# Neighbourhood attention and MLP on one core: x and the result held by channel, 16-bit row maxima through a step-zero column

## What is computed

```python
h1 = n1_w * arcsinh(x) + n1_b
h  = x + na2d(h1)                      # qkv, softmax over 9 neighbours, projection
h2 = n2_w * arcsinh(h) + n2_b
out = h + gelu(h2 @ mlp_w1 + mlp_b1) @ mlp_w2 + mlp_b2

def na2d(x):
    q, k, v = split(x @ qkv_w + qkv_b)
    scores = einsum('bijnd,bijmnd->bijnm', q * hd**-0.5, k[neighbours])
    return einsum('bijnm,bijmnd->bijnd', softmax(scores), v[neighbours]) @ proj_w + proj_b
```

## Time and profile before

| | |
|---|---|
| median of 3 runs | 4412.26 us |
| profiled execution: span | 4410.1 us |
| TensorE matmul busy | 4291.9 us (97%) |
| TensorE weight loads busy | 3082.4 us (70%) |
| VectorE busy | 3769.7 us (85%) |
| ScalarE busy | 3660.2 us (83%) |
| GpSimd busy | 3450.6 us (78%) |
| granted TensorE clock, mean | 0.992 |
| DMA, mean | 136 GB/s |

### The profile page before, as it was taken

The page is one execution under the profiler, slowest core; times in us unless marked ns, Lnnn a source line. Parts: engine busy times, 40 slices in busy tenths (PEclk is TensorE's granted clock), DMA queues, the critical chain, the costliest instruction groups (busy, mean ns, idle before and its releaser), DMA issues.

```text
span 4410.1 us, 136683 instructions
## 1 busy us (share of the span) xinstructions
PE 4291.9 (97%) x53320; PEld 3082.4 (70%) x53320; DVE 3769.7 (85%) x7715; ACT 3660.2 (83%) x5377; POOL 3450.6 (78%) x4092
## 2 busy tenths in 40 slices
PE   5999999999999999999999999999999999999997
PEld 3677777767777777776777777777777767777775
DVE  5888888888888888888888888888888888888884
ACT  4888888888888888888888888888888888888884
POOL 2787887888788788888878878887887888788775
PEclk8999999999999999999999999999999999999998
DMA  4555555555555555555555555555555555555551
GB/s 118 130 137 144 136 139 139 141 140 138 140 140 137 143 136 139 139 139 140 138 144 135 138 141 139 140 138 142 136 138 139 140 139 139 141 139 137 140 134 51
DMA packets 593555, 600.06 MB, mean 136 GB/s; under 512 B 76558, under 2 KB 540560, under 8 KB 590352
## 3 DMA queue, kind: packets, MB, share of 16 engines
q1 hardware_dynamic: 592912, 591.32, 51.4%
HBM read 197.69 MB, written 135.40 MB: 76 GB/s over the span
## 4 chain that ended last, share of the span: by engine, by line
DVE 42%; PE 34%; issue 12%; POOL 11%; SPq 1%; ACT 1%; DMA 0%; POOLq 0%; DVEq 0%; ACTq 0%
PE ps L382 32%; DVE ln_u L777 8%; DVE ln_u L773 8%; POOL a_lo L1162 6%; DVE o_norm L882 6%; DVE ps L851 5%; POOL a_hi L1160 3%; DVE q_nat L818 2%; DVE y L845 2%; DVE recip L873 2%; DVE v_nat L832 2%; PE ps L406 2%; DVE o_lo L838 2%; DVE ln_u L770 1%; DVE maxima L857 1%
## 5 line engine op out<-in xcount | busy, mean ns | idle before, releaser
L1154 POOL TENSOR_TENSOR p_lo<-prob,p_hi 100x512 f16<-100x512 f32 x1024 | 1256.7, 1232 | 639.1 <-ACT p_hi L1072 639.1
L1071 ACT ACTIVATE prob<-ps 100x512 f32<-100x512 f32 x1024 | 613.6, 599 | 143.2 <-PE ps L382 141.8
L882 DVE TENSOR_TENSOR o_norm<-ps,recip 64x128 f32<-64x128 f32 x2048 | 591.3, 289 | 49.4
L1180 POOL TENSOR_TENSOR g_lo<-g,g_hi 128x512 f16<-128x512 f32 x512 | 595.9, 1164 | 41.0
L1072 ACT ACTIVATE p_hi<-ps 100x512 f16<-100x512 f32 x1024 | 617.2, 603 | 0.0
L382 PEld LDWEIGHTS ps<-v_win,p_hi 100*128 100x128 f16 x8192 | 484.7, 98 | 185.3 <-issue 15.3
L851 DVE TENSOR_REDUCE ps<-ps 128x8 f32<-128x800 f32 x512 | 509.5, 995 | 88.9 <-PE ps L382 84.8
L382 PE MATMUL ps<-w_hi,g_hi 128*128 128x256 f16 x2048 | 560.3, 274 | 0.0
L382 PE MATMUL ps<-w_lo,g_hi 128*128 128x256 f16 x2048 | 560.2, 274 | 0.0
L382 PE MATMUL ps<-w_hi,g_lo 128*128 128x256 f16 x2048 | 560.1, 273 | 0.0
L382 PE MATMUL ps<-v_win,p_hi 100*128 100x65 f16 x8192 | 516.5, 194 | 26.0 <-POOL p_lo L1154 15.8
(11 more groups left out here) (103 smaller groups left out, 11981.0 us busy)
## 6 DMA issues: line engine op xcount, KB each, us to landing
keys<-k_win SPq DMA_DIRECT2D x1536, 100.0 KB, 2.2
v_win<-v_rows SPq DMA_DIRECT2D x1024, 101.6 KB
queries<-q_nat SPq DMA_DIRECT2D x1536, 64.0 KB
v_rows<-v_nat SPq DMA_DIRECT2D x256, 260.0 KB, 5.6
xin<-in_x_dram SPq DMA_DIRECT2D x128, 512.0 KB, 4.5
out_dram<-y SPq DMA_DIRECT2D x256, 256.0 KB, 3.1
queries<-in_query_mask_dram SPq DMA_DIRECT2D x128, 160.0 KB
keys<-in_mlp_w_dram SPq DMA_DIRECT2D x2, 512.0 KB, 7.5
```

The lines of the kernel that those rows point to most:

```text
L882: s = v.tensor_tensor(o_norm[r, c], av[r, :, HD * e:HD * e + HD], recip[c % 2][r].to_broadcast([NQ, PAIRS, HD]), ALU.mult)
L1071: act.activation(prob[b][0:NK], ps[0:NK, B_ST + b, :], ACT.Exp, scale=INV * INV).then_inc(prob_ready, 1)
L1154: pool.tensor_tensor(p_lo[b][0:NK], prob[b][0:NK], p_hi[b][0:NK], ALU.subtract).then_inc(p_lo_ready, 1)
L1180: pool.tensor_tensor(g_lo[:, m, :], g32[:, m, :], g_hi[:, m, :], ALU.subtract).then_inc(g_lo_ready, 1)
```

## The change

x reaches the device with channels on partitions: the host lays it out as (band, 128, 2, 512), and takes the result back in the same form. The eight x transposes, their copies and the eight transposes of h are gone; x is no longer held times 16. A load goes straight into one of five `xT` buffers (before: four, and one input buffer). `mlp_out` makes the result with channels on partitions, 24 matmuls of 512 columns, with the weight as the stationary operand; h is added by VectorE, in `result`, after `h_plus_bias` has added the bias to it in place. The banks of v, of the result and of the waits on them are handed out anew. The projection weight's scale goes from 16 to 4, and its counterpart, the ones beside v, from 1 to 4.

VectorE writes the maxima as one bf16 number in SBUF, and `subtract_max` multiplies a stationary operand that is one column read 128 times (step zero) with minus the identity. The second bf16 part, the transpose and the copy are gone.

```diff
-XT = 4
+XT = 5
-X_BANK = [1, 0]
-V_BANK = [2, 1]
-OUT_BANK = [2, 0]
+V_BANK = [1, 2]
+OUT_BANK = [0, 2]
...
-                if has(t + 4):
-                    sp.wait_ge(pe_x, signals(t + 3, G, G))
+                if t >= 0 and has(t + 4):
+                    if has(t - 1):
+                        sp.wait_ge(h_ready, signals(t - 1, G, G))
                     load_x(t + 4)
...
             def v_product(t, n):
-                if n == 0:
+                if n == 1:
                     pe.wait_ge(q_lo_ready, signals(t, G, 1))
-                elif has(t + 1):
-                    pe.wait_ge(xT_ready, signals(t + 1, G, 1))
-                else:
+                elif has(t - 3):
                     pe.wait_ge(h_ready, signals(t - 3, G, 2))
...
             def mlp_in(t, m):
                 if m == 0 and has(t - 1):
+                    pe.wait_ge(y_ready, signals(t - 1, 2, 2))
+                elif m == 0:
+                    pe.wait_ge(v_lo_ready, signals(t + 3, 2, 2))
+                elif m == 1 and has(t - 1):
                     pe.wait_ge(y_ready, signals(t - 1, 2, 1))
-                elif m == 0:
-                    pe.wait_ge(v_lo_ready, signals(t + 3, 2, 1))
-                elif m == 1 and has(t - 1):
-                    pe.wait_ge(y_ready, signals(t - 1, 2, 2))
...
-            def mlp_out(t, par, n):
+            def mlp_out(t, g):
...
-                for k in range(2):
-                    tok = slice((2 * n + k) * P, (2 * n + k + 1) * P)
-                    o = ps[:, OUT_BANK[n], k * C:(k + 1) * C]
-                    for g in range(G):
-                        pe.matmul(o[:, g * P:(g + 1) * P], h[par][:, g, tok], ident[:], start=(k == 0 and g == 0),
-                                  stop=False, is_transpose=True, skip_group_check=True)
-                    for m in range(MT):
-                        s = three(o, [g_[:, m, tok] for g_ in (g_hi, g_lo)], [w[:, m, :] for w in (w2_hi, w2_lo)],
-                                  False, m == MT - 1)
+                for m in range(MT):
+                    s = three(ps[:, OUT_BANK[g], :], [w[:, m, g * P:(g + 1) * P] for w in (w2_hi, w2_lo)],
+                              [g_[:, m, :] for g_ in (g_hi, g_lo)], m == 0, m == MT - 1)
                 s.then_inc(pe_m2, 1)
...
-                    s = mm(ps[:, B_ST + c % 2, p * P:(p + 1) * P], key_max[:, (c % 2) * PAIRS + p, :], max_row[k % 2][:],
-                           stop=True)
+                    a = maxima[k % 2][:, c % 2, p:p + 1]
+                    column = bass.AP(a.tensor, a.offset, [list(a.ap[0]), [0, P]])
+                    s = mm(ps[:, B_ST + c % 2, p * P:(p + 1) * P], column, minus_ident[:], stop=True)
...
             def magnitude_plus_root(u, root, s):
-                v.scalar_tensor_tensor(out=u, in0=u, scalar=INV, in1=root, op0=ALU.mult, op1=ALU.add).then_inc(s, 1)
+                v.tensor_tensor(u, u, root, ALU.add).then_inc(s, 1)
...
-            def result(t, n):
-
-                v.wait_ge(pe_m2, signals(t, 2, n + 1))
-                v.wait_ge(y_out[n], signals(t, 16, 0))
-                v.scalar_tensor_tensor(out=y[n][:], in0=ps[:, OUT_BANK[n], :].rearrange("p (k c) -> p k c", c=C), scalar=INV,
-                                       in1=b2[:].rearrange("p (a c) -> p a c", a=1).to_broadcast([P, 2, C]),
+            def h_plus_bias(t, par):
+                v.wait_ge(asinh2, signals(t, 1, 1))
+                for g in range(G):
+                    v.tensor_scalar(h[par][:, g, :], h[par][:, g, :], b2[:, g:g + 1], None, ALU.add).then_inc(hb_ready, 1)
+
+            def result(t, par, g):
+
+                v.wait_ge(pe_m2, signals(t, 2, g + 1))
+                v.wait_ge(y_out[g], signals(t, 16, 0))
+                v.wait_ge(hb_ready, signals(t, G, g + 1))
+                v.scalar_tensor_tensor(out=y[g][:], in0=ps[:, OUT_BANK[g], :], scalar=INV, in1=h[par][:, g, :],
                                        op0=ALU.mult, op1=ALU.add).then_inc(y_ready, 1)
```

More of the change, by code:

```diff
@@ L158, in build @@
         p_lo = [sb(f"p_lo{i}", [P, 512], F16) for i in range(2)]
-        maxima = [sb(f"maxima{i}", [P, P], BF16) for i in range(2)]
-        max_row = [sb(f"max_row{i}", [P, P], BF16) for i in range(2)]
+        maxima = [sb(f"maxima{i}", [P, 2, PAIRS], BF16) for i in range(2)]
         recip = [sb(f"recip{i}", [P, PAIRS, 1], F32) for i in range(2)]
@@ L171, in build @@
         g_hi, g_lo = sb("g_hi", [P, MT, TOK], F16), sb("g_lo", [P, MT, TOK], F16)
-        y = [sb(f"y{i}", [P, 2, C], F32) for i in range(2)]
+        y = [sb(f"y{i}", [P, TOK], F32) for i in range(G)]
         stage = keys[:].rearrange("p i k -> p (i k)").bitcast(F32)
@@ L389, in three @@
                 return mm(o, al, bh, stop=stop)
-            def x_transposes(t, g):
-                if g == 0:
-                    pe.wait_ge(x_in, signals(t, 16, 16))
-                    if has(t - 4):
-                        pe.wait_ge(h_ready, signals(t - 4, G, 2))
-                    else:
-                        pe.wait_ge(k_lo_ready, signals(t - 1, G, 1))
-                else:
-                    pe.wait_ge(q_lo_ready, signals(t - 1, G, 2))
-                x_matmuls(g)
-            def x_matmuls(g):
-                for k in range(BLOCKS):
-                    s = pe.transpose(ps[:, X_BANK[g], k * P:(k + 1) * P], xin[:, k, g * P:(g + 1) * P], ident[:])
-                s.then_inc(pe_x, 1)
             def k_product(t, g):
@@ L555, in scores @@
                 s.then_inc(pe_s, 1)
-            def max_rows(t, k):
-                pe.wait_ge(max_ready, signals(t, SLOTS, k + 1))
-                pe.transpose(ps[:, B_S, MAXT_COLS].bitcast(BF16), maxima[k % 2][:], ident16[:]).then_inc(pe_max, 1)
             def scores_t(t, par, c):
@@ L680, in step @@
                         weighted(t, par, 2 * k)
-                    if more:
-                        max_rows(ahead[0], ahead[2])
                     if k == 0 and post:
@@ L897, in opening @@
                     zero(v_nat[:, 1].rearrange("p a w -> p (a w)"))
[L898 removed]
+                    zero(v_nat[:, 0].rearrange("p a w -> p (a w)"), PS)
                 else:
@@ L941, in step @@
                         sign1(t + 3, (u + 3) % XT)
+                    if k == 3 and post:
+                        h_plus_bias(t - 1, old)
                     if att:
@@ L965, in step @@
                     if k == 2 and fin:
-                        result(t - 2, 0)
+                        result(t - 2, par, 0)
                     if att:
@@ L975, in step @@
                     if k == 2 and fin:
-                        result(t - 2, 1)
+                        result(t - 2, par, 1)
             for t_ in queries:
                 zero(t_[:].rearrange("p n g c q -> p (n g c q)").bitcast(U32), 0)
-            for t_ in (*maxima, *max_row):
-                zero(t_[:])
             for t in range(-3, 0):
@@ L1239 @@
     arrays, args = {}, []
-    given = [(n, np.ascontiguousarray(inputs[n if n == "x" else "L0_conv_" + n])) for n in _INS]
+    x = np.asarray(inputs["x"]).reshape(BANDS, TOK, G, P).transpose(0, 3, 2, 1)
+    given = [(n, np.ascontiguousarray(x if n == "x" else inputs["L0_conv_" + n])) for n in _INS]
     for name, a in given + list(constants().items()):
```

180 lines of the change are left out of this document (64 added, 116 removed).

## The result

The changed kernel takes 4478.7 us (median of 4 runs, 4476.8 to 4478.9), the kernel before, beside it on the same chip, 4411.8. The ratio is 1.0149, with a 95% interval of 1.0135 to 1.0162. The prediction was 4375 us, with a range of 4285 to 4440. It is wrong in sign and outside its range.

The account below looks back on a forecast made before the run. VectorE's stretch to y(1) holds `mlp_in(0)` until 18.76 us into the band; with 14.47 behind it the period is 33.23, 0.27 less. 4410.1 - 34 - 3 = 4373, median 2.2 higher: 4375 us, range 4285 to 4440.

Parts of the forecast that it names:

- The clock: TensorE over the whole run: the granted clock does not fall in mid run in spite of the 2.3 us wait.
- The new wait: TensorE at `mlp_in(0)`, now behind y(1), VectorE's last operation of slot 2: waits about 2.3 us a band.
- Root2 and the start of sum2: Slot 1, from S (its `subtract_max` start): root2 still ends at S+6.78, sum2 starts at S+6.84, 0.55 us earlier.
- Contention: VectorE beside GpSimd, sum2 to y(1): net +0.2 us, bounds -1.5 and +1.3, so y(1) ends at S+18.71.
- TensorE's rest: From `mlp_in(0)` to the next S: TensorE bounds, 14.74 less two maxima transposes (0.12) and the 0.15 wait, 14.47 us.
- The ends: Setup and last bands, where x and h transposes stand on the chain: 3 us saved, an estimate.
- Maxima and step-zero column: `subtract_max` keeps its time, eight in 0.61; 32 step-zero loads a band cost nothing, bounds 0 to 0.53 us a band.
- `h_plus_bias`: VectorE ahead of o_norm(6): the pair takes 0.72 us undisturbed, hidden before `weighted(7)` with 0.4 us to spare.
- the third rival: GpSimd slows `h_plus_bias`, so `weighted(7)` starts 0.44 us later: period 33.67, 4431 us; decides above 1.1 us together; 15%.
- The form of the sums: sum1 and sum2 as plain additions on VectorE: no change taken, bounds nothing and a 0.1 gain.
- The first: TensorE's whole saving comes out, the wait on y(1) does not bite: 300 us less, 4110 us; 5%.
- four sums: Less contention: 4285 or 4330, 16%; slowed `h_plus_bias`: 4431, 15%; 0.25 us more contention: no change, 10%; forecast: 4375, 46%.

Follow-up runs that it names:

- Experiment 5: Changed kernel with `h_plus_bias` removed, the bias entering as one more TensorE product of 512 columns per half: 4482.2 us, 1.016 against the kernel before.
- experiment 7: Changed kernel, `mlp_in(0)` waiting for y(0) instead of y(1): 4330.1 us; also with bias as TensorE product: 4272.9; also with `v_low(0)` ahead of sum2: 4305.9.
- experiment 6: Changed kernel with sum1 and sum2 back in the earlier kernel's scalar-tensor-tensor form, factor 1.0: 4479.6 us, 1.0152 against the kernel before.

## Why the prediction was wrong, by its steps

- **The clock.** "The granted clock does not fall in mid run in spite of the wait": this is the step that failed. I saw that TensorE would stand still for 2.3 us a band, where it had no wait over about 0.3, and put no price on it; no rival had one either. In place of a clock that stays, the runs show one that falls to 0.50 for some 3 us in every second band. The runs with 16 and 32 filling matmuls, and with 4 and 8 beside them, give the price: 100 of the 104 us between forecast and result. With the 16, which shorten the wait and do no useful work, the kernel takes 4379.
- **The new wait.** Right in place, releaser and size (2.29 against 2.3).
- **Root2 and the start of sum2.** Root2 ends at 2237.07, S+6.78 as predicted; sum2 starts at S+6.87 (6.84).
- **Contention.** +0.2 was predicted, +0.44 came: sum2's start to the end of y(1) takes 12.11 where 11.67 was the undisturbed sum. By its parts: sum2 2.17, 0.95 more, which I had left at its 1.22 while moving its start by half a microsecond, onto g_lo (2237.09 to 2238.25); sign2 1.53, 0.3 more where I wrote 0.9, since p_lo(5) came at S+11.18 but sign2 only at S+11.89, and 0.46 of the two overlap; magnitude1 0.68 (0.75 predicted), 0.97 less; sum1 2.04, 0.25 more (0.2 predicted). That is 0.54 together; the small maxima operations gave back 0.42 and not the 0.29 that I took (from the start of the reduce to that of sign2 1.31 before, 0.89 now). So y(1) ends at S+18.98, not S+18.71.
- **TensorE's rest** 14.29 (2284.27 to 2298.56) against 14.47. The step that was short is the wait for `a_lo`, which I took at the 0.15 that the row shows as idle. Idle time counts from the modelled end of the last matmul. From the start of the transposes in front to that of `k_product` it is 0.81 before (2225.89 to 2226.70) and 0.49 without the wait (2291.68 to 2292.17): 0.32. The undisturbed period is 33.33 against 33.23: 13 us too little over 126 bands. The ends saved about 10 us, not 3: 4412 less 126 x 0.18 is 4389, and the kernel with 16 takes 4379. The two misses nearly cancel (4375 against 4379); that is luck.
- **Maxima and step-zero column.** Right: loads 98 ns, products 220 ns, eight in 0.61; the maxima alone are worth 59 us.
- **`h_plus_bias`.** The pair takes 2.13 us, far over the 1.1 from which the third rival was to decide, and yet `weighted(7)` does not wait. The pair costs 1.4 more than the undisturbed 0.72. Some 0.9 of it comes back at sign1, for which the prediction had 2.1 (S+20.2 to 22.3) beside p_lo(7), and which takes 1.21 now, while p_lo(7) takes 2.20. The rest comes out of the 0.4 us that the prediction had to spare and out of TensorE's coming 0.3 later than 24.3. o_norm(6) ends at 2289.60, 0.23 before TensorE is there (VectorE, then TensorE):

```profile
2289.01 0.59 DVE L812 TENSOR_TENSOR o_norm<-ps,recip 64x128 f32<-64x128 f32 x2
2289.83 0.23 PE L369 MATMUL ps<-v_win,p_hi 100*128 100x65 f16 x2
```

  Experiment 5 shows that it is off the path, experiment 7 that it is on it as soon as the wait in front shrinks.
- **The form of the sums.** It was right to take nothing for it (experiment 6). No run shows the 0.1 that the prediction had as a bound.
- **Rivals.** The first (all of TensorE's saving) was rightly held unlikely. The forecast side had four sums that differed in contention and waits, and none in which a wait makes the work behind it slower; that one decided.

## What to carry to other kernels

A wait of TensorE has two prices: its length, and what the clock does behind it. When a change gathers a band's slack into one wait, ask how long that one wait becomes: here 1.5 us was free of the second price, 1.7 almost, and 1.9 cost as much as 2.3 (0.8 us a band on average). Look at the mean granted clock and at successive periods, not at one band. Measure a short wait from start to start against a band without it, not by the idle time of the row. Then fill the wait, split it, or better take away its cause; and try an edit that "is worth nothing" again after the wait in front of it has gone.

## What the hardware showed that I had not expected

- A single wait of 1.9 to 2.3 us of a TensorE that is busy for nearly all the rest of a 33 us band takes the granted clock from 1.00 to 0.50 for some 3 us, in every second band at a period of 33.3 us and in about every third at 34.7; the matmuls stretch at once or up to 1.3 us after TensorE is back at work. Two waits of 1.67 and 0.67 in a band did it in 6 of 128 bands, and a wait of 1.51 in none.
- sum2 took 1.22, 1.63, 1.66, 1.90, 2.05 or 2.17 us in these kernels, at one shape, as its start moved by tenths of a microsecond against GpSimd's work. The one that starts second loses. In the traces of the fourteen kernels, away from their ends, a sum or sign of 1024 columns on VectorE and a subtraction on GpSimd (p_lo, g_lo, a_lo, b_lo) overlap by over 0.3 us, with no second subtraction beside it, some 5600 times: each time the one that started first kept its time, and the other was stretched. So sign1 takes 1.86 before, from 2221.08, behind a p_lo(7) from 2220.70; in the changed kernel it starts at 2250.68, 0.02 ahead of p_lo(7), keeps its 1.21, and p_lo(7) takes 2.20. Of two operations that will meet, see to it that the one on the path starts first.
- The loads of a stationary operand with step zero take the same 98 ns as any 16-bit one.
